# Self-attention queries and keys built into the score stacks through DRAM instead of by TensorE transposes

## The reference, cut to what matters

```
q, k = rope(x @ wq.T), rope(x @ wk.T)            # 16 heads of 16
x1 = layernorm(x + softmax(q k^T / 4) v)
x2 = layernorm(x1 + (softmax(mask(q2 k2^T / 4)) v2) @ Wo.T + bo)   # q2 from x1, k2 and v2 from ctx
gates = softmax(x2 @ router_w);  top 2, each expert takes the first CAP tokens
out = layernorm(x2 + sum of gate * expert(x2))
```

## Time and profile before

| | |
|---|---|
| median of three runs (range) | 2275.64 us (2265.10 to 2276.37) |
| the profiled execution: its own time | 2272.11 us |
| its span, first to last instruction | 2270.4 us |
| mean granted TensorE clock | 0.965 of full |
| busy: TensorE, VectorE, ScalarE, GpSimd | 95%, 53%, 44%, 26% |
| first duo of self-attention | at 15.5 us |
| one step in the steady state (two slots) | 47.4 us |
| last work of attention; first of the experts | 1634 us; 1643 us |

### The profile page before, as it was taken

The page is one execution under the profiler, slowest core; times in us unless marked ns, Lnnn a source line. Parts: engine busy times, 40 slices in busy tenths (PEclk is TensorE's granted clock), DMA queues, the critical chain, the costliest instruction groups (busy, mean ns, idle before and its releaser), DMA issues. The chain is left out here.

```text
span 2270.4 us, 48602 instructions
## 1 busy us (share of the span) xinstructions
PE 2163.7 (95%) x18846; PEld 1506.0 (66%) x18846; DVE 1200.3 (53%) x2522; ACT 1004.9 (44%) x1538; POOL 601.0 (26%) x937
## 2 busy tenths in 40 slices
PE   7899999999999999999999999999799999999990
PEld 4566666666666666666666666666478778787780
DVE  3466676766767767777677776764111111111114
ACT  1355555555555555555555555553231222212225
POOL 2113222332223322233222332222212122121223
PEclk6899999999999999999999999998799999999995
DMA  6311111211101110011000010000113332333217
GB/s 179 105 29 31 35 31 49 65 36 62 34 27 36 37 30 24 22 28 34 28 25 23 27 34 24 27 20 13 37 35 84 77 68 36 82 84 77 24 17 303
DMA packets 97666, 115.72 MB, mean 51 GB/s; under 512 B 12096, under 2 KB 91021, under 8 KB 95392
## 3 DMA queue, kind: packets, MB, share of 16 engines
q1 hardware_dynamic: 68112, 82.38, 11.7%
q0 software_dynamic: 17664, 18.35, 5.2%
q10 hardware_dynamic: 11664, 11.88, 1.8%
HBM read 64.53 MB, written 56.05 MB: 53 GB/s over the span
## 5 line engine op out<-in xcount | busy, mean ns | idle before, releaser
L867 DVE TENSOR_REDUCE smax<-ps_s 128x4 f32<-128x1024 f32 x500 | 609.3, 1219 | 311.3 <-PE ps_s L574 265.8
L753 ACT ACTIVATE prob<-ps_e 128x1024 f32<-128x1024 f32 x500 | 511.9, 1024 | 525.6 <-PE ps_e L583 403.6
L574 PE MATMUL ps_s<-stack 17*128 17x256 f32 x4000 | 573.7, 404 | 26.6 <-DVE smax L867 21.1
L583 PE MATMUL ps_e<-stack 18*128 18x256 f32 x4000 | 572.4, 404 | 6.9 <-DMA stack<-nrows 5.1
L574 PEld LDWEIGHTS ps_s<-stack 17*128 17x128 f32 x4000 | 347.8, 186 | 207.8 <-issue 115.8
L583 PEld LDWEIGHTS ps_e<-stack 18*128 18x128 f32 x4000 | 344.6, 186 | 12.2 <-DMA stack<-nrows 7.1
L1534 ACT ACTIVATE hid<-m_ps_h,b_sb 128x320 f32<-128x320 f32 x256 | 135.0, 527 | 415.5 <-PE m_ps_h L1494 415.5
L1494 PE MATMUL m_ps_h<-m_cols,w_sb 128*128 128x320 f32 x1024 | 293.1, 435 | 0.6 <-DVE m_cols L1551 0.6
L1511 PE MATMUL m_ps_o<-w_sb,hid 128*128 128x256 f32 x1280 | 278.9, 379 | 0.0
L1511 PEld LDWEIGHTS m_ps_o<-w_sb,hid 128*128 128x128 f32 x1280 | 243.2, 190 | 34.8
L599 PE MATMUL ps_w<-prob,val 128*32 128x256 f32 x4096 | 257.5, 394 | 1.7 <-ACT prob L753 1.7
(11 more groups left out here) (134 smaller groups left out, 2241.8 us busy)
## 6 DMA issues: line engine op xcount, KB each, us to landing
w_sb<-in_w SPq DMA_DIRECT2D x16, 1024.0 KB, 6.4
slot_rows_dram<-fill ACTq DMA_DIRECT2D x8, 1290.0 KB, 10.7
m_rows<-slot_rows_dram SPq DMA_DIRECT2D x16, 645.0 KB, 4.7
xT<-in_xT SPq DMA_DIRECT2D x32, 256.0 KB, 2.8
ctxT<-in_ctxT SPq DMA_DIRECT2D x32, 256.0 KB, 2.8
x_res<-in_x SPq DMA_DIRECT2D x32, 256.0 KB, 3.1
stack<-nrows SPq DMA_DIRECT2D x512, 2.0 KB
sums_dram<-x SPq DMA_DIRECT2D x32, 256.0 KB, 2.2
```

The costliest lines, as they stand in the source:

```text
L574: mm = nc.tensor.matmul(scores[:, p % 2, t, :], stack[X][rows, Q, p // HG, t * P:(t + 1) * P], stack[X][rows, K, p // HG, :], start=True, ...
L583: mm = nc.tensor.matmul(shifted[:, p % 2, t, :], stack[Y][rows, K, h // HG, t * P:(t + 1) * P], stack[Y][rows, Q, h // HG, :], start=True, ...
L753: nc.scalar.activation(prob[:, h:h + 2, :].rearrange("p h s -> p (h s)"), shifted[:, :, :, :].rearrange("p h t s -> p (h t s)"), ACT.Exp, ...
L867: nc.vector.tensor_reduce(max_columns(X, p), scores[:, :, :, :], AX.X, ALU.max)\
```

## The change

Self queries and keys no longer pass `padded`, the TensorE transposes and the ScalarE copies.

- **Projection.** The self weights are reordered on chip at the start (`turn_columns`: eight VectorE copies), so that `project(SELF, ...)` yields queries or keys in columns at once: four pieces of four matmul records with 256 columns each; before, four pieces of two records with 512 columns. Cosine and sine are widened and transposed once (`widen_rope`).
- **Turning.** `turn(b, part)` does the same three VectorE operations on one part (Q or K) instead of on one half of the tokens; GpSimd adds (`turned_part`).
- **Through DRAM.** SyncE writes each part with two DMAs of 128 KB (`write_part`) and reads each half of the stacks with two of 256 KB (`read_half`). Mask row and zero rows are written to DRAM once.
- **Order.** The beside work of TensorE, ScalarE and VectorE is laid out anew; the self values are computed at C3, not S7; the second half of `second_norm` moves from C6 to C7, `shares` and `choose` from C4 to C0, `gates` from C1 to C0, `routing_logits` from C0 to S7. GpSimd keeps its order, except that the self sum is split over both slots.
- **Start.** The weights that are needed later are loaded only after both halves of the first stack have come; the zero rows for routing (nine DMAs of 1.3 MB by ScalarE) go out every third duo from step 1, not every duo from slot C of step 0.

```diff
+        def write_part(eng, b, part):
+            eng.wait_ge(turned_made.sem, turned_made.count(b, part + 1))
...
+            for c in range(2):
+                eng.dma_start(rows[:, STRIP * c:STRIP * (c + 1), part, :], turned[:, part, c, :]).then_inc(written[part].sem, 16)
+        def read_half(eng, b, half):
+            for part in (Q, K):
+                eng.wait_ge(written[part].sem, written[part].count(b))
...
+            if e_mm[SELF].due(b - 1, 4 * half + 4):
+                eng.wait_ge(e_mm[SELF].sem, e_mm[SELF].count(b - 1, 4 * half + 4))
+            for part in (Q, K):
+                eng.dma_start(stack[SELF][:, part, 2 * half:2 * half + 2, :],
+                              DRAMS.image[:, 2 * half:2 * half + 2, part, :]).then_inc(stack_in[half].sem, 16)
```

VectorE, after the reduction of each duo:

```diff
+            def beside_self(i, m):
...
+                if m == 0 and there(i - 3):
+                    second_normed(i - 3)
+                if m == 1 and there(i - 1):
+                    divide(SELF, i - 1, 0)
+                    divide(SELF, i - 1, 1)
+                    first_sum(i - 1)
+                if m == 2 and there(i - 1):
+                    mean_and_variance(SELF, i - 1, 6, y, stats)
+                if m == 3:
+                    if there(i - 1):
+                        first_normed(i - 1)
+                    if there(i + 1):
+                        turn(i + 1, Q)
+                if m == 4 and there(i - 1):
+                    cross_part(i - 1, 0)
+                if m == 5 and there(i - 1):
+                    cross_part(i - 1, 1)
+                if m == 7 and there(i - 3):
+                    routing_logits(i - 3)
+            def beside_cross(i, m):
+                if m == 0 and there(i - 3):
+                    shares(i - 3)
+                    choose(i - 3)
+                if m == 1 and there(i + 1):
+                    turn(i + 1, K)
+                if m == 2 and there(i - 2):
+                    divide(CROSS, i - 2, 0)
+                    divide(CROSS, i - 2, 1)
+                if m == 3 and there(i):
+                    values(SELF, i)
+                if m == 5 and there(i - 3):
+                    positions(i - 3)
+                if m == 6 and there(i - 2):
+                    second_sum(i - 2)
+                if m == 7:
...
+                        values(CROSS, i - 1)
...
+                        mean_and_variance(CROSS, i - 2, 5, y2, stats2)
...
+                        own_positions(i - 3)
```

More of the change, by code:

```diff
@@ L95, in __init__ @@
     def __init__(self):
-        self.slots = self.sums = None
+        self.slots = self.sums = self.image = None
     def make(self, nc):
@@ L236, in attend @@
         consts = steps("consts", 2)
+        image_made = steps("image_made", 4 * 16)
+        weights_turned = both("weights_turned", 4)
+        rope_wide_made = steps("rope_wide_made", 2 * T2)
+        rope_mm = steps("rope_mm", 1)
+        rope_made = steps("rope_made", 1)
+        written = [steps("written_" + part, 2 * 16) for part in "qk"]
+        stack_in = [steps("stack_in_" + half, 2 * 16) for half in "01"]
         filled = steps("filled", 7)
@@ new lines, in widen_rope @@
+            def widen_rope():
+                pe.wait_ge(rope_wide_made.sem, rope_wide_made.count(0))
+                for of in range(2):
+                    for t in range(T2):
+                        mm = nc.tensor.transpose(ps_e[:, 0, of, t * P:(t + 1) * P], rope_wide[:, of, t, :], ident[:, :])
+                mm.then_inc(rope_mm.sem, 1)
+            widen_rope()
+            project(SELF, 0, 0)
+            project(SELF, 0, 1)
+            project(SELF, 0, 2)
+            project(SELF, 0, 3)
@@ new lines, in beside_cross @@
+            def beside_cross(i, m):
+                if m == 0 and there(i - 3):
+                    gates(i - 3)
+                if m == 1 and there(i - 1):
+                    stack_columns("stack_k", CROSS, i - 1, 1)
+                if m == 2 and there(i - 1):
+                    stack_columns("stack_q", CROSS, i - 1, 1)
+                if m == 5:
+                    if there(i - 1):
+                        max_rows(CROSS, i - 1, 0)
+                    if there(i - 2):
+                        columns(CROSS, i - 2)
@@ L836, in _ @@
+            for half in range(2):
+                read_half(act, 0, half)
             slots_of(emit, act)
@@ L1094, in _ @@
+            dve.wait_ge(rope_mm.sem, rope_mm.count(0))
+            nc.vector.tensor_copy(rope[:, :, :], ps_e[:, 0, :, :]).then_inc(rope_made.sem, 1)
+            dve.wait_ge(rope_made.sem, rope_made.count(0))
+            turn(0, Q)
+            turn(0, K)
             slots_of(emit, dve)
```

516 lines of the change are left out of this document (273 added, 243 removed).

## The result

| | before | after |
|---|---|---|
| median of four runs (range) | 2274.31 us (2265.10 to 2276.37) | 2302.01 us (2296.47 to 2307.73) |
| the profiled execution: its own time | 2272.11 us | 2300.3 us |
| its span | 2270.4 us | 2298.3 us |
| mean granted TensorE clock | 0.965 | 0.960 |

A forecast was written before the change was run, and what follows sets the result against it. TensorE's order of work was taken to bound the steps. Steady state 0, steps 1 to 3 -5, pipeline's end -2 and start +7 summed to 0 on the profiled 2272.1 us: forecast 2272, range 2225 to 2303.

The forecast's parts named there:

- start, to S0 of step 1: Longer preparation and later weights before the first duos, less a vanished wait for maxima in step 0: net +7 us.
- steps 1 to 3: Early steps, where no scatter and no shares stand in the way: 3 x -1.8, counted as -5 us.
- steps 4 to 30: Steps with routing and scatter: -2.0 us from TensorE, given back by three delays of 0.5, 0.3 and 1.2; net 0.
- pipeline's end: Some slots at the pipeline's end, where the same saving was expected: -2 us.
- S4: Duo 4 of the self slot: GpSimd's backlog delays the first norm, so 4.7 us instead of 3.53, +1.2 a step.
- C1: Duo 1 of the cross slot: VectorE's shares wait for gates, so 3.1 us instead of 2.6, +0.5 a step.
- The third term: Passage from cross to self slot: VectorE's cross values and second-norm statistics lengthen the first self duo to 3.2 us, +0.3.
- (a): Rival for the steady state: none of the three delays shows, 2217 us; chance 0.10.
- (b): Rival for the steady state: delays are half those counted, GpSimd being free in time, 2238 us; chance 0.26.
- Rival (c): New SyncE traffic delays the maxima's DMAs, 0.5 us at two duos in every step: +31, 2303 us; chance 0.17.
- Rival (d): TensorE's clock falls after the 1.2 us wait in each of 28 steps: +48, 2320 us; chance 0.04.
- My margin of 0.3 us at S5: Maxima DMAs at self duo 5: with about 2.0 us fixed per transfer, 0.3 us remains and still holds.

The follow-up runs named there:

- fills aside: Changed kernel with the nine zero-row fills sent three at the end of step 0, then one at duo 4 of each slot: 0.9692 at the slow place, 1.0098 at the first.
- after_silent: Changed kernel with each indirect DMA of the scatter replaced by a GpSimd power that sends nothing: 2312.12 us, 1.0165 of the kernel before.

## Why the prediction was wrong

The terms of my sum against the traces:

| part | forecast | measured |
|---|---|---|
| start, to S0 of step 1 | +7 | +5.7 |
| steps 1 to 3 | -5 | +15.9 |
| steps 4 to 30 | 0 | +6.1 |
| pipeline's end, to the first work of the experts | -2 | +0.8 |

**The step that failed: steps 1 to 3, and the fills in them.** I wrote that in the slot C of step 0 "the zero rows no longer crowd the maxima", and counted -5 for steps 1 to 3. I looked at where the fills went away from and not at where they went to: into steps 1 and 2, nine fills of 1.3 MB beside the same small DMAs. I had even read the price, 4.38 us at the first C4. Instead of -3.6 steps 1 and 2 cost +16.7, an error of 20 us. With the fills aside (at the first place) the three waits vanish, and the value products of S0 in steps 1 and 3 are 9.7 and 12.6 us behind the kernel before instead of 6.6 and 22.4. So the two steps lose 3 us instead of 16, while 3 are lost sooner: S0 of step 1 waits 2.77 us for ScalarE, which issues three fills just before. The fills are thereby shown as the cause of 13 us within the steps, of which my new placing of them paid 3 again; a gain of 9 to 11 us at step 3 came out of all three pairs of traces.

The steps then still lose 3 where I forecast a gain of 3.6. The traces put this rest in step 1: with the fills aside step 2 takes 45.9 us against 47.4 before, nearly the gain I forecast, but step 1 takes 54.9 against 49.5. TensorE works at the 1.2 GHz level in parts of it (0.84 and 0.80 in the two windows shown above), as in C3, where this product takes 1.99 us at full clock:

```profile
112.04 3.75 PE L528 MATMUL ps_w<-wv,xT 128*128 128x256 f32 x8
```

Why step 1 stays slow no run here separates. Nor was the old placing better for the changed kernel (slow place): with it the fills held up the maxima and the read of the stack, and S0 of step 3 came 5 us later still.

**The steady state: the sum was nearly right, its largest term by the mechanism I gave.** Forecast 47.4, measured 47.58. S4 took 4.50 (4.7 forecast), GpSimd being free only after the scatter: the late scatter took it to 3.53. C1 took 2.93 (3.1), because VectorE waited for `gates` ahead of `shares`; with `gates` at C1 and `shares` at C4 again it took 2.68. The third term came to nothing: S0 took 2.94, its length by TensorE alone, where I had 3.2; VectorE began S0's reduction 1.53 us behind the duo, and I had counted 1.9. Two small terms I didn't have: S7 2.85 (2.53), where C0's duo waited 0.25 us for ScalarE's copy of the stack group, and with the copy earlier waited for VectorE instead; and C2 2.78 (2.52), which `shares` at C4 brings to 2.63. They make up for what I counted too much. Over 27 steps the 0.15 us are 4 us; the jump at 1100 us and smaller ones bring it to 6.1.

**The pipeline's end** lost 0.8 us where I had counted a gain of 2; this was not looked into by any run.

**Rivals (a) and (b)** fell: the wait for GpSimd was there in every step, 1.42 us in the one shown, where (b) had it vanish. **Rival (c)** had the right collision at the wrong place: 0.5 us in each step was refuted by the steady state itself, which shows no such wait, and by four more DMAs a step without one; 2.7 to 3.2 us three times in steps 1 and 2 were real. My margin of 0.3 us at S5 took a figure for GpSimd's DMAs over to DMAs that SyncE sends, and no run tested it. **Rival (d)** was small at most: in one step, at 1108.6 us, two duos behind an S4 of 4.50, the clock went to the 1.2 GHz level and S7 took 4.01 instead of 2.85. With an S4 of 4.88 (after_silent) such jumps came in four steps, to some 6 us in all. That S4's wait sets them off is likely from this, not shown.

**The start: right in sum, wrong in its parts.** First duo 26.76 for 21.3, first C0 50.66 for 45.5, but S0 of step 1 +5.7 for +7. The write and the read through DRAM with what surrounds them took 11.9 us from the end of GpSimd's last addition (14.86) to the first duo, where I had 6.6 by rows that stand mostly for the steady state: the read was issued only at 21.35. That earlier weights don't help in the end was measured.

**The range** held the time, by 1 us at its upper end, and that was luck: the end was set by rival (c), a wait in every step, and most of the measured loss came from two steps at the start.

## What to carry to other kernels

When large transfers are moved away from one place, price the place they come to by the same row that priced the one they left, and look there for small DMAs that the bounding engine waits for. A microsecond taken from the engine that bounds comes back only if no other engine's written order ends later: here I had counted 2 us a step out of TensorE, and a gain appeared (1.2 us a step) only when GpSimd's scatter and VectorE's shares were put behind what TensorE waits for.

## What the runs showed of the hardware

**A wait at the end of indirect DMAs that one place has and the other has not.** The same kernel took 2441 and 2273 us. At the slow place VectorE stood idle behind a finished duo of TensorE for 2.6 and 2.7 us in the two steps shown, until 1.2 us after the end of GpSimd's fourth indirect DMA, and took the first of these duos 3.1 us later than usual; ScalarE stood idle beside it. Moving the scatter moved the wait, and without the scatter the wait was gone and the changed kernel fell from 2386 to 2263. At the first place leaving the sending out changed 0.2%. It turned the sign of the result of this change: 0.9775 and 1.0137. A trace of one place does not show which of the two a kernel will meet.

**The clock fell behind waits of 2.4 to 3 us**: the value product took 3.58 instead of 1.93 after [2.40 <-DVE smax] (fills aside, slow place). Behind the waits of 2.68 and 3.23 us in steps 1 and 2 of the changed kernel, first records took 0.80 us, and the products ahead of both waits had run at full clock (1.03); ahead of the one of 2.85 it was low already (2.08). After waits of 0.80 us, at 110.35 and 150.56, the first records took 0.48. The Trainium skill ("TensorE: Matmul & The Clock Gate", section "A second HAM failure mode: psum-queue depth-cycling") says that micro-idles alone can make the clock swing. In the changed kernel's steady state, with two waits of 0.4 us in each S4, I saw it clearly once, at 1108 us.
